# The softmax maximum as three bfloat16 words with new orders in the attention pipeline, and the second block table in two parts with longer register loads

## What is computed

```python
x = x + xattn(layernorm(x), ctx, pos, pos)        # 64 batches of 64 tokens, 32 heads of width 8
#   q = rope(xn @ Wq), k = rope(ctx @ Wk), v = ctx @ Wv
#   w = softmax(q k^T / sqrt(8)); out = (w v) @ Wout + bout
x = x + ffn(layernorm(x))                         # 8 experts, the best 2 of each token
#   scores = xn @ Wg^T; top 2; shares = softmax of the two scores
#   y = sum over the two of share * (silu(xn @ W1[e]^T) * (xn @ W2[e]^T)) @ W3[e]^T
```

## Time and profile before

| what | us |
|---|---|
| time before, median of 3 runs | 529.66 (529.56 to 529.92) |
| the profiled execution, its time | 529.24 |
| the profiled execution, its span | 527.3 |
| PE busy in the span | 474.1 (90%) |
| DVE busy | 405.5 (77%) |
| POOL busy | 366.0 (69%) |
| ACT busy | 351.6 (67%) |

### The profile page before, as it was taken

The page is one execution under the profiler, slowest core; times in us unless marked ns, Lnnn a source line. Parts: engine busy times, 40 slices in busy tenths (PEclk is TensorE's granted clock), DMA queues, the critical chain, the costliest instruction groups (busy, mean ns, idle before and its releaser), DMA issues.

```text
span 527.3 us, 21533 instructions
## 1 busy us (share of the span) xinstructions
PE 474.1 (90%) x7701; PEld 365.8 (69%) x7701; DVE 405.5 (77%) x1199; ACT 351.6 (67%) x929; POOL 366.0 (69%) x634
## 2 busy tenths in 40 slices
PE   3676899999999999999999999889899999899890
PEld 2563566676676766767666665559799999889780
DVE  7376689899898999999989898767655556776672
ACT  3473677877778777777777777667466666566550
POOL 4442758888888888888888887356666557675471
PEclk9787999999999999999999999899899999999895
DMA  6920101121121212212111110143654446877844
GB/s 192 235 71 7 30 20 54 40 74 43 60 66 49 94 52 70 65 48 67 40 61 56 50 35 25 44 120 96 195 158 132 127 127 202 251 236 240 303 146 159
DMA packets 43225, 54.55 MB, mean 103 GB/s; under 512 B 6727, under 2 KB 36849, under 8 KB 43122
## 3 DMA queue, kind: packets, MB, share of 16 engines
q1 hardware_dynamic: 36066, 35.79, 24.5%
q0 software_dynamic: 6480, 16.85, 8.9%
q10 hardware_dynamic: 576, 0.53, 0.3%
HBM read 29.60 MB, written 23.94 MB: 102 GB/s over the span
## 4 chain that ended last, share of the span: by engine, by line
PE 69%; DVE 12%; DMA 6%; issue 6%; SPq 2%; ACT 2%; POOL 2%; POOLq 0%; DVEq 0%; ACTq 0%
PE logit_banks L1551 9%; PE bank L1401 6%; PE logit_banks L1570 6%; PE logit_banks L1361 6%; PE logit_banks L1342 5%; PE bank L1388 5%; PE qkv_banks L1310 5%; PE logit_banks L1369 5%; PE bank L1394 4%; PE qkv_banks L1321 3%; DVE negmax L757 3%; PE qkv_banks L1301 3%; DMA y_in<-result_rows 3%; PE bank L1331 3%; PE bank L1539 2%
## 5 line engine op out<-in xcount | busy, mean ns | idle before, releaser
L691 POOL DMA_INDIRECT result_rows<-blocks_io,blk_dest x71 | 72.5, 1021 | 53.3 <-ACT blocks_io L1245 23.8
L657 POOL DMA_INDIRECT routed_rows<-xs,slots x64 | 65.7, 1026 | 16.7 <-issue 16.7
L757 DVE TENSOR_REDUCE negmax<-logit_banks 128x16 f32<-128x1024 f32 x64 | 75.0, 1212 | 2.3 <-PE logit_banks L1342 2.3
L1137 ACT ACTIVATE late<-logit_banks 128x1024 f32<-128x1024 f32 x64 | 62.0, 1021 | 14.4 <-PE logit_banks L1369 14.4
L664 POOL TENSOR_TENSOR ropes<-rope_a,ropes 128x512 f32<-128x512 f32 x32 | 41.2, 1288 | 29.5 <-DVE ropes L744 29.5
L1022 DVE TENSOR_TENSOR gated<-xn,logit_banks 128x176 f32<-128x176 f32 x71 | 23.8, 335 | 46.8 <-ACT xn L1251 45.8
L764 DVE RECIPROCAL rden<-bank 128x256 f32<-128x256 f32 x32 | 55.8, 1745 | 0.8 <-PE bank L1394 0.8
L648 POOL TENSOR_TENSOR mid<-mid,mask 128x512 f32<-128x512 f32 x44 | 44.7, 1035 | 11.8 <-ACT mid L1118 11.7
L1551 PE MATMUL logit_banks<-w_hi,x_hi 128*128 x142 | 47.0, 331 | 0.0
L1551 PE MATMUL logit_banks<-w_hi,x_lo 128*128 x142 | 46.4, 327 | 0.0
L1251 ACT ACTIVATE xn<-logit_banks 128x176 f32<-128x176 f32 x71 | 22.5, 316 | 35.7 <-PE logit_banks L1551 35.7
(11 more groups left out here) (219 smaller groups left out, 1378.8 us busy)
## 6 DMA issues: line engine op xcount, KB each, us to landing
blocks_io<-routed_rows SPq DMA_DIRECT2D x71, 129.0 KB, 2.4
y_in<-result_rows SPq DMA_DIRECT2D x16, 512.0 KB, 4.6
x_sb<-in_x_dram SPq DMA_DIRECT2D x32, 128.0 KB, 2.1
out_dram<-o_sb SPq DMA_DIRECT2D x16, 256.0 KB, 3.8
ctx_sb<-in_ctx_dram SPq DMA_DIRECT2D x32, 64.0 KB, 2.3
blocks_io<-in_L_ffn_W_dram SPq DMA_DIRECT2D x4, 512.0 KB, 6.8
mid<-mT SPq DMA_DIRECT2D x128, 4.0 KB
routed_rows<-pad_row SPq DMA_DIRECT2D x11, 129.0 KB, 2.9
```

What stands on the lines that cost most here:

```text
L657: nc.gpsimd.indirect_dma_start(routed[:, :], bass.IndirectOffsetOnAxis(ap=slots[:, t.slot(TR), k:k + 1], axis=0), xs[:, t.slot(TR), k, :], ...
L691: nc.gpsimd.indirect_dma_start(results[:, :], bass.IndirectOffsetOnAxis(ap=blk_dest[:, b.slot(RB):b.slot(RB) + 1], axis=0), y_sb[:, b.slot ...
L757: V.tensor_reduce(negmax[:, t.par, 16 * half:16 * half + 16], ps_s[:, 1024 * half:1024 * half + 1024].rearrange("p (h k) -> p h k", k=N), ...
L1137: S.activation(pT[:, 1024 * half:1024 * half + 1024], ps_s[:, 1024 * half:1024 * half + 1024], ACT.Exp, scale=SCALE).then_inc(exp_done, 1)
```

## The change

**The maximum as three words.** `peak` writes the maximum into the first third of `negmax`. A new stage on POOL, `split_max` of c+1, takes from it what its upper 16 bits hold, which read as a bfloat16 number, and writes the rest as a second word, and from that in the same way a third; the two subtractions hang on each other by a semaphore. `transpose_max` now moves 96 rows and waits for `split_max`, `mT` has 96 rows, each of the four DMAs writes three rows, and the eight matmuls of L1369 multiply three rows with ones in bfloat16.

**New orders.** On PE `project_v` goes ahead of the shifted logits, `transpose_max` behind them, and `rank` from behind them to behind `project_out`; `transpose_x` goes ahead of `project_out`. On DVE `invert_sums` and `normalise_attn` go ahead of the routing, which is now in one piece. On ACT `copy_v` goes ahead of `copy_mT` and `normalise_x1` behind `copy_xT`. The results of `rank` move to another PSUM bank, so `attend` waits for `rank_read`, and `residual` for `rank_done`.

**The second table in two parts.** `rest_blocks` runs twice: once for the first 28 tiles, in turns 30 and 31 and between the first operations of the expert layer, which gives blocks 17 to 48 (`MID` is 49), and once for all tiles, in blocks 14 to 17, for blocks 49 to 70. SP fetches the first part behind the load of block 7 and the second behind that of block 27; the padding moves from behind block 11 to behind block 15.

**Longer register loads.** SP loads 17 and then 18 row numbers at a time; PE loads 17 and then 21 expert numbers at a time, ahead of blocks 17, 35 and 53.

```diff
@@ maximum
+        def maxima(par, part, r=slice(0, RG)):
+            return negmax[:, par].rearrange("p (r s h) -> p r s h", r=RG, s=3)[:, r, part]
+        def leading(par, part):
+            return negmax[:, par].bitcast(BF16).rearrange("p (r s h w) -> p r s h w", r=RG, s=3, w=2)[:, :, part, :, 1]
...
+            def split_max(t):
+                pool.wait_ge(max_done, t.times(2, 2))
+                nc.gpsimd.tensor_tensor(maxima(t.par, 1), maxima(t.par, 0), leading(t.par, 0), ALU.subtract)\
+                    .then_inc(parts_step, 1)
+                pool.wait_ge(parts_step, t.n + 1)
+                nc.gpsimd.tensor_tensor(maxima(t.par, 2), maxima(t.par, 1), leading(t.par, 1), ALU.subtract)\
+                    .then_inc(parts_done, 1)
...
-                    row = slice(32 * r, 32 * r + 1)
+                    row = slice(32 * r, 32 * r + 3)
...
-                        ins = M.matmul(banks[r][64 * c:64 * c + 64, :], ones_row[row, :],
-                                       ms[row, :].rearrange("p (g c k) -> p g c k", c=KC, k=N)[:, :, c, :],
+                        ins = M.matmul(banks[r][64 * c:64 * c + 64, :], ones_bf[row, 0:N],
+                                       ms[row, :].bitcast(BF16).rearrange("p (g c k w) -> p g c k w", c=KC, k=N, w=2)[
+                                           :, :, c, :, 1],
@@ orders: POOL, DVE, PE
                     pair(t)
+                do(split_max, t.plus(1))
                 do(normalise_x, t.plus(4))
...
                 do(peak, t.plus(1))
+                do(invert_sums, t.plus(-1))
+                do(normalise_attn, t.plus(-1))
                 do(best_scores, t.plus(-2))
                 do(best_experts, t.plus(-2))
                 do(mark_choices, t.plus(-2))
                 do(join_choices, t.plus(-2))
-                do(invert_sums, t.plus(-1))
-                do(normalise_attn, t.plus(-1))
                 do(place_tokens, t.plus(-2))
...
                 do(transpose_kq, t.plus(2))
+                do(project_v, t.plus(1))
+                do(shifted_logits, t)
                 do(transpose_max, t.plus(1))
-                do(shifted_logits, t)
+                do(project_k, t.plus(3))
+                do(transpose_x, t.plus(4))
+                do(project_out, t.plus(-1))
                 do(rank, t.plus(-2))
-                do(project_k, t.plus(3))
-                do(project_v, t.plus(1))
-                do(project_out, t.plus(-1))
                 do(project_q, t.plus(3))
-                do(transpose_x, t.plus(4))
@@ tables and register loads
+                if t.c >= T2 + 2:
+                    rest_blocks(t.c - T2 - 2, NG - 1, mid_done)
...
-                rest_blocks(b.c - JOIN)
+                if b.c >= 2 * JOIN:
+                    rest_blocks(b.c - 2 * JOIN, NG, rest_done)
...
-            row_starts, row_counts = chunks(RB)
+            row_starts = [0, FULL, 2 * FULL + 1, 3 * FULL + 2, NBLK]
...
-                if c == RB + 3:
+                if c == RB - 1:
+                    sp.wait_ge(mid_done, 2)
...
+                if c == FULL - 2:
                     for e, rows in enumerate(load_counts(sp, 0)):
                         pad_expert(sp, e, rows)
-                if c == FULL - 3:
+                if c == JOIN + 20:
                     sp.wait_ge(rest_done, 2)
...
-            exp_starts, exp_counts = chunks(4)
+            exp_starts = [FULL, 2 * FULL + 1, 3 * FULL + 2]
...
+                count = min(FULL + 4, (FULL if first == 0 else NBLK) - first)
```

More of the change, by code:

```diff
@@ L326, in xattn_ffn_kernel @@
         gap_done, lean_done = sem("gap_done"), sem("lean_done")
-        full_in, rest_in = sem("full_in"), sem("rest_in")
+        full_in, mid_in, rest_in, mid_done = (sem(s) for s in ("full_in", "mid_in", "rest_in", "mid_done"))
         wg_done, wg_sb = sem("wg_done"), sem("wg_sb")
@@ L407, in blocks @@
                 body(do, Turn(0, c, RB))
-        def chunks(step):
-            starts = list(range(0, FULL - step // 2, step)) + list(range(FULL, NBLK, step))
-            return starts, [end - start for start, end in zip(starts, starts[1:] + [NBLK])]
         def group_of(v):
@@ L515, in _ @@
             back = results.rearrange("(v p r) d -> v p (r d)", p=P, r=4)
-            row_starts, row_counts = chunks(RB)
-            row_regs = [sp.alloc_register(f"row{n}") for n in range(max(row_counts))]
+            row_starts = [0, FULL, 2 * FULL + 1, 3 * FULL + 2, NBLK]
+            row_regs = [sp.alloc_register(f"row{n}") for n in range(FULL + 1)]
             rows_of = {}
@@ L755, in peak @@
                 dve.wait_ge(s_done, t.n + 1)
+                wait_past(dve, mT_done, t.n - 1)
                 for half in range(2):
-                    V.tensor_reduce(negmax[:, t.par, 16 * half:16 * half + 16],
-                                    ps_s[:, 1024 * half:1024 * half + 1024].rearrange("p (h k) -> p h k", k=N),
+                    V.tensor_reduce(maxima(t.par, 0, slice(2 * half, 2 * half + 2)),
+                                    ps_s[:, 1024 * half:1024 * half + 1024].rearrange("p (r h k) -> p r h k", r=2, k=N),
                                     AX_X, ALU.max, negate=True).then_inc(max_done, 1)
@@ L980, in full_blocks, with rest_blocks @@
                     V.tensor_scalar(full_i[:, 1:2], full_exp[:], float(E - 1), None, ALU.min).then_inc(full_done, 1)
-            def rest_blocks(step):
+            def rest_blocks(step, ng, done):
                 flat = "p g e -> p (g e)"
+                n = ng * E
                 if step == 0:
-                    whole(ups[:].rearrange(flat), cnts[:].rearrange(flat), UP)
+                    whole(ups[:, 0:ng].rearrange(flat), cnts[:, 0:ng].rearrange(flat), UP)
                     V.tensor_copy(prior[:, 0], full_cnt[:])
-                    tab(V.tensor_copy(prior[:, 1:NG], ups[:, 0:NG - 1]))
+                    tab(V.tensor_copy(prior[:, 1:ng], ups[:, 0:ng - 1]))
@@ L1006, in rest_blocks @@
[L1006 to L1007 removed]
+                    if ng == NG:
+                        dve.wait_ge(mid_in, 32)
+                    V.tensor_tensor(rest_i[:, 0:1], rest_row[:], rest_base[:], ALU.add).then_inc(done, 1)
+                    V.tensor_reduce(rest_exp[:], seg_past[:, 0:n], AX_X, ALU.add)
+                    tab(V.tensor_reduce(seg_over[:], seg_past[:, 0:n].rearrange("p (g e) -> p g e", e=E)[:, :, E - 1],
+                                        AX_X, ALU.add))
@@ L1347, in transpose_max @@
             def transpose_max(t):
-                pe.wait_ge(max_done, t.times(2, 2))
+                pe.wait_ge(parts_done, t.n + 1)
                 wait_past(pe, mT_sb, t.n)
+                pe.wait_ge(rope_done, upto(t.n + 2))
+                pe.wait_ge(gate_x_done, upto(t.n + 2))
                 M.transpose(ps_mT, negmax[:, t.par, :], ident[:]).then_inc(mT_done, 1)
@@ L1510, in body @@
                     transpose_weights(range(6, 8))
-            exp_starts, exp_counts = chunks(4)
-            ahead = [[pe.alloc_register(f"expert{k}_{n}") for n in range(max(exp_counts))] for k in range(2)]
+            exp_starts = [FULL, 2 * FULL + 1, 3 * FULL + 2]
+            ahead = [pe.alloc_register(f"expert{n}") for n in range(FULL + 4)]
             experts = {}
             def load_experts(first):
-                k = exp_starts.index(first)
-                if first == 0:
-                    pe.wait_ge(full_in, 32)
-                if first == FULL:
-                    pe.wait_ge(rest_in, 32)
-                regs = ahead[k % 2][:exp_counts[k]]
-                pe.load(regs, exp_i[0:1, first:first + exp_counts[k]])
-                for n, reg in enumerate(regs):
+                count = min(FULL + 4, (FULL if first == 0 else NBLK) - first)
+                pe.wait_ge(*{0: (full_in, 32), FULL - 3: (mid_in, 32)}.get(first, (rest_in, 32)))
+                pe.load(ahead[:count], exp_i[0:1, first:first + count])
+                for n, reg in enumerate(ahead[:count]):
                     experts[first + n] = pe.snap(reg, min_val=0, max_val=E - 1)
```

82 lines of the change are left out of this document (42 added, 40 removed).

## The result

The changed kernel takes 554.98 us (median of 4 runs, 554.01 to 557.44), the kernel before 529.79: a ratio of 1.048, 95% interval 1.045 to 1.052. The forecast was 545.7, so the sign is right and the size 9.3 us too small. The profiled execution took 554.01 us; its span, 552.1, is 24.8 longer than that of before.

What follows compares the result with a forecast made beforehand. PE's own work was taken to bound the 9.36 us turn, with DVE and POOL close behind. Terms 18.6 + 2.7 - 1.0 - 0.3 - 4.0 = +16.0 on 529.66 gave 545.7 us, range 535 to 560.

Steps and rivals of the forecast that it cites:

- PE: 0.33 us for the matmuls of the maximum: Attention turn on PE: L1369 falls from 1.00 to 0.33 us, PE's own turn from 9.36 to 8.7.
- POOL: 0.6 us for the subtractions, masks at 6.5 to 8.55: Attention turn on POOL: two subtractions add 0.6 us (bounds 0.4 and 2.0), its sum becomes 9.5, the masks move later.
- The ring of 9.75: Attention turn: DVE's residual, POOL's rotation, PE up to rank, then place to DVE's turn end sum to 9.75 us.
- Routing behind the masks, a turn of 10.05: Attention turn: DVE's later routing waits out POOL's masks, turn 9.95 to 10.15, +18.6 us over turns 2 to 28; case A 0.54.
- the two cases that I had named: DVE's routing: gap ends with the first mask, onehot with the second, chosen at 8.8; or gap and onehot together, chosen 8.6.
- First table, +2.7: Attention: the first table's 12 operations lie on DVE's path, 3.0 us with gaps, where they cost some 0.3 before.
- End of attention, -0.3: Turn 29 -2.6, turn 31 +1.4, load of 17 experts in turn 30 +0.6, last steps of the first part +0.3.
- Expert layer, -4.0: Expert layer: 4.5 us gained at block 12, 0.8 given back at block 17, 0.3 gained on register loads.
- The gain at block 12: Expert layer: PE's wait for block 12 behind SP's paddings, with half clock and a load of experts, goes: 4.5 us.
- even and odd: Register loads of four numbers: 0.34 us where the first number's place is even, 1.02 where it is odd.
- a rival with that price: Rival F, expert layer: register loads go by the odd price, 0.25 us a number; with A 555; chance 0.08.
- SP's reading: Expert layer: 18 row numbers take SP 3.8 us, 2.1 more than eight; 0.8 given back for block 17 (bounds 0 and 2.1).

Runs made afterwards that it cites:

- the run with three words: Kernel before plus the three-word maximum and POOL's subtractions, old orders but for two moves, tables of before: 535.85 us, ratio 1.016.
- The maximum alone: Kernel before plus the maximum in three words and the new orders, nothing of the tables: 541.54 us, ratio 1.025.
- the tables alone: Kernel before plus the second table in two parts and the long register loads, nothing of the maximum and orders: 539.65 and 543.40 us.
- the last run: Changed kernel with register loads beginning at multiples of four and SP's paddings moved behind the load of block 13: 539.41 us.

## Why the prediction was right in sign and short in size

The direction and the mechanism in attention held. That the time came as near as 9.3 us is in part luck: the two largest terms missed by 8.7 us in one direction and by 13 in the other.

- **PE: 0.33 us for the matmuls of the maximum.** 0.50 in three words (151.66 to 152.16; the eight begin within some 0.2 us and last 0.39 each, so they run beside one another), 0.36 in one. The step was roughly right; PE was not the bound anyway.
- **POOL: 0.6 us for the subtractions, masks at 6.5 to 8.55.** 0.55, and masks at 6.26 to 8.30: the rotation starts 0.1 us earlier (2.22), and from its start to the masks it is 4.04 us instead of 3.58, only 0.46 more, since POOL's gaps were smaller.
- **The ring of 9.75.** It is 9.49 in the run without subtractions, where PE has no idle time from the rotation to `rank`: PE's part there is 4.63 us where I summed 4.8, and the rotation ends at 3.49, not 3.62.
- **Routing behind the masks, a turn of 10.05.** The mechanism holds in the steady turn: `gap` and `onehot` got through at the first mask's end, one of the two cases that I had named, and `chosen` was held to the end of the second. But that end came at 8.30 instead of 8.55, by the two points above, and I had taken the middle of the two cases. The sum with what was measured, 8.32 + 0.30 + 1.06 = 9.68, is the turn. This mis-sized term makes 27 x 0.37 = 10 us too much; the first table gives some of it back, and 8.7 is left in turns 2 to 28. Three rows with inputs in SBUF alone end with a mask: `chosen` (0.89) here, `seen` (0.74) in the run with three words and `gap` (0.67) in the one without the subtractions.
- **First table, +2.7.** Turns 15 to 20 are 6.5 us longer than before, 4.6 of them more than six ordinary turns (6 x 0.33): in turn 16 two operations of the table, L991 and L992, take 0.66 and 0.62 us instead of 0.17, the first ending behind POOL's second operation of the scatter (L675), the second with `add_bias` (L650), and in the same turn `onehot` is held for 1.09. I had counted the operations and not what they meet.

```profile
215.06 0.66 DVE L991 TENSOR_TENSOR full_cnt<-full_end 128x8 f32<-128x8 f32 x1
215.75 0.62 DVE L992 TENSOR_SCALAR full_skip<-full_cnt 128x8 f32<-128x8 f32 x1
```

```profile
214.61 0.97 POOL L675 DMA_INDIRECT routed_rows<-xs,slots  x1 [0.30 <-issue]
215.60 0.73 POOL L650 TENSOR_TENSOR xres<-x_sb,bout_sb 128x256 f32<-128x256 f32 x1
```

- **End of attention, -0.3.** Turn 29 came out as forecast (8.94 for 8.9). The rest cost 5.9 instead of 2.3: 1.4 in turn 30, 3.1 in turn 31, 1.4 behind. The maximum alone loses 1.0 in turn 31 and 2.4 in turn 32, so a part that I had left out is the new orders' cost in the last turns; the tables alone lose 2.3 in turns 30 to 32, about what I had priced.
- **Expert layer, -4.0.** This step failed, by 13 us: it came to +9.0. The gain at block 12 was nearly right (3.9 for 4.5). The price of a register load was read from rows at places 4, 8 and 17, 21, ...: cheap and dear, and I took even and odd for the cause. 14 and 50 are even and dear; 0, 4, 8, 12, 16, 20, 24, 32 and 48 are cheap. Multiples of four is what the runs bear out. So two of three loads on PE and three of four on SP went at 0.22 to 0.29 us a number; the case had a rival with that price, at 8 in 100, and its 555 is what came, though by a smaller sum in attention and a larger one here, so that hit is luck, too. The cheap loads take 0.07 to 0.1 us a number.
- **SP's reading** of 18 numbers was priced right for block 17 (3.8; 4.01 measured), but the block's lateness was not: I gave back 0.8 us (bounds 0 and 2.1), and PE waited 4.00. What I did not price is SP's later reading: its 5.15 us at 474.0 stand ahead of a load of results that DVE waits for inside its queue, and the stops of PE are followed by stretches at half the clock (0.57 from 404 to 408, 0.50 from 488 to 492).

## What to carry over

Price a register load by the place in its table at which it begins (23 numbers from place 12 took 2.10 us here, 21 from 14 took 5.18), and count who stands behind it on the engine that reads: a long load on an engine that issues transfers stops everyone who waits for these (SP read for 4.01 us ahead of block 17, and PE waited 4.00). Work added to an engine with little slack costs less by its own length than by what it pushes to a place where another engine's operations meet it (here `chosen`, held for 0.89 us, to the end of the mask); and where one ring is taken away, look for the next (without the subtractions the turn fell by 0.18 us, not by the 0.55 that they take). Before a number is carried at full precision, ask whether it cancels: here the leading bits were enough, and the two added operations not needed.

## What the runs showed of the hardware

- A register load took 0.07 to 0.1 us a number where it began at a multiple of four in its row (23 numbers: 2.10 us; eight: 0.53), and 0.2 to 0.29 elsewhere (21: 5.18; eight: 1.67). Some short ones from aligned places lie above this (in the kernel before, four from place 0 0.52, five from 12 0.79). Some loads late in the kernel took longer at either place (19 aligned numbers 3.16, 23 from 48 2.81 in one run and 2.09 in another, four from an odd place 2.59 in the kernel before); why is not shown.
- Of three operations of DVE in a row, each with two inputs in SBUF, `gap` (0.20 us) and `onehot` (0.16) got through where POOL's first mask ended, at 153.27, and `chosen` took 0.89, to the end of the second mask; it takes 0.24 where no mask runs beside it.
- With PE idle for 0.56 and 0.23 us in each turn of 9.67, the clock was granted in full through all of attention (1.00 from 68 to 333 us). In the expert layer of the changed kernel it fell to half behind the stops of 4.00 and 3.21 us (0.57 from 404 to 408, 0.50 from 488 to 492); behind the 1.6 us lost at block 34 (451 to 455), and behind the 1.65 and 1.93 left in the last run (394.7 to 410), it stayed in full (1.00).
